# Value matmuls of 64-wide heads on four parts of the array, with an output projection split by sequence

## The reference

```python
q = (query @ Wq).reshape(Bq, Sq, 16, 64).transpose(0, 2, 1, 3)
k = (key @ Wk).reshape(Bq, Sq, 16, 64).transpose(0, 2, 1, 3)
v = (value @ Wv).reshape(Bq, Sq, 16, 64).transpose(0, 2, 1, 3)
scores = jnp.einsum('bhqd,bhkd->bhqk', q, k) / jnp.sqrt(64)
attn = jax.nn.softmax(scores, axis=-1)       # its window is wider than the 64 tokens
out = jnp.einsum('bhqk,bhkd->bhqd', attn, v)
return out.transpose(0, 2, 1, 3).reshape(Bq, Sq, 1024) @ Wo
...
x = x + jnp.tanh(g_xattn[3]) * _L3_xattn_ref(_layernorm(x), ctx_1024, ctx_1024, ...)
```

## Time and profile before

| what | value |
|---|---|
| median of 3 runs | 4556.94 us (4556.47 to 4561.93) |
| profiled execution | 4552.95 us, its span 4551.1 us |
| mean granted clock of TensorE | 0.866 |
| PE busy, matmuls | 3947.3 us (87%) |
| PE busy, weight loads | 3104.3 us (68%) |
| DVE busy | 3006.2 us (66%) |
| ACT busy | 1735.9 us (38%) |
| POOL busy | 764.9 us (17%) |

### The profile page before, as it was taken

One profiled execution on the slowest core, in us unless ns is written; L12 is line 12 of the kernel. 1 busy time (PEld: TensorE's weight loads), 2 busy tenths in 40 slices (PEclk: granted clock), 3 DMA queues, 4 the chain that ended last, 5 costly groups with the idle time before them and its releaser, 6 DMA issues.

```text
span 4551.1 us, 105680 instructions
## 1 busy us (share of the span) xinstructions
PE 3947.3 (87%) x36890; PEld 3104.3 (68%) x36890; DVE 3006.2 (66%) x9082; ACT 1735.9 (38%) x4156; POOL 764.9 (17%) x575
## 2 busy tenths in 40 slices
PE   6999978888886888889999999777737899999965
PEld 4888855555554555589999999655537777777754
DVE  4666657777775777766666666799861355555569
ACT  3555534444442344333333333222203344444421
POOL 1222221111110000011111111100171122222211
PEclk9999987777776677689999999888758999999975
DMA  3000010000001000000000000100015200000000
GB/s 124 8 7 8 7 23 6 6 6 6 6 7 65 16 16 15 15 6 0 0 0 0 0 0 3 44 12 12 6 39 191 98 12 12 9 12 12 10 13 26
DMA packets 102053, 97.04 MB, mean 21 GB/s; under 512 B 31664, under 2 KB 91056, under 8 KB 101296
## 3 DMA queue, kind: packets, MB, share of 16 engines
q1 hardware_dynamic: 97408, 76.94, 5.6%
q0 software_dynamic: 4096, 8.40, 0.6%
q10 hardware_dynamic: 432, 10.19, 0.6%
HBM read 46.97 MB, written 19.66 MB: 15 GB/s over the span
## 4 chain that ended last, share of the span: by engine, by line
PE 60%; DVE 18%; SPq 8%; issue 7%; POOL 2%; DMA 2%; ACT 1%; DVEq 1%; POOLq 0%; ACTq 0%
PE ps L768 54%; SPq L591 7%; PE ps L936 5%; DVE acc L1658 2%; DMA arena_a<-kT 1%; DVE o_sb L1637 1%; POOL scr L718 1%; PE ps L806 1%; DVE arena_b L1606 1%; POOL route L740 1%; DVE xn L1442 1%; DVE x_sb L1557 1%; DVE st L1401 1%; DVE mx L1527 1%; DVE vsmall L1614 1%
## 5 line engine op out<-in xcount | busy, mean ns | idle before, releaser
L768 PE MATMUL ps<-xcT,small 128*128 128x256 f32 x2176 | 610.1, 419 | 34.7 <-DMA xcT<-in_ctxT 25.4
L732 POOL TENSOR_TENSOR rstd<-veps,neghalf 128x2 f32<-128x2 f32 (+1 forms) x224 | 167.9, 749 | 2403.8 <-DVE veps L1434 2071.2
L768 PEld LDWEIGHTS ps<-xcT,small 128*128 128x128 f32 x2176 | 411.3, 204 | 233.3 <-issue 114.5
L768 PE MATMUL ps<-arena_b,qT 64*64 64x64 f32 (+3 forms) x11136 | 541.8, 242 | 21.6 <-DVE arena_b L1606 20.3
L1278 ACT ACTIVATE kT<-ps 128x256 f32<-128x256 f32 (+1 forms) x768 | 294.4, 383 | 623.6 <-PE ps L768 547.4
L768 PE MATMUL ps<-small,xcT 128*64 128x64 f32 (+5 forms) x3072 | 482.7, 384 | 51.4 <-DVE acc L1658 30.3
L768 PE MATMUL ps<-xhi,parts_a 128*128 128x256 f32 (+1 forms) x2112 | 500.4, 289 | 22.7 <-DVE qT L1687 22.7
L768 PEld LDWEIGHTS ps<-arena_b,qT 64*64 64x64 f32 (+3 forms) x11136 | 463.5, 149 | 58.4 <-issue 35.0
L1248 ACT ACTIVATE pT<-ps 128x512 f32<-128x512 f32 (+1 forms) x576 | 303.3, 571 | 467.0 <-PE ps L936 465.3
L1687 DVE TENSOR_TENSOR qT<-kT,ps 128x256 f32<-128x256 f32 (+1 forms) x768 | 316.8, 419 | 188.5 <-ACT kT L1278 181.0
L768 PE MATMUL ps<-xlo,parts_a 128*128 128x256 f32 (+1 forms) x1536 | 430.6, 280 | 0.0
(11 more groups left out here) (212 smaller groups left out, 6388.5 us busy)
## 6 DMA issues: line engine op xcount, KB each, us to landing
wbuf<-parts_b SPq DMA_DIRECT2D x39, 512.0 KB, 3.0
arena_a<-kT SPq DMA_DIRECT2D x1024, 8.0 KB
xcT<-in_ctxT SPq DMA_DIRECT2D x96, 128.0 KB, 2.1
xn<-scr SPq DMA_DIRECT2D x39, 128.0 KB, 2.2
scr_y<-acc SPq DMA_DIRECT2D x39, 128.0 KB, 2.9
scr<-vsmall SPq DMA_DIRECT2D x9, 512.0 KB, 13.3
ctx_sb<-in_ctx SPq DMA_DIRECT2D x32, 128.0 KB, 2.1
arena_a<-in_w ACTq DMA_DIRECT2D x1, 4096.0 KB, 12.4
```

The source lines that it names most:

```text
L732: pool.tensor_tensor(rstd[:, 0:n], veps[:, 0:n], neghalf[:, 0:n], ALU.pow).then_inc(s_rstd.sem, 1)
L768: return nc.tensor.matmul(o, lhsT, rhs, start=start, stop=stop, skip_group_check=True)
```

## The change

In both layers the value matmuls now run in one loop over heads, row half and sequence. The row half (which heads) decides the bank, and half and sequence together decide the output rows: for hb = 0 the rows are those of the half, for hb = 1 the other ones. So oT of the second sequence holds the even and odd heads with their row halves exchanged. ACT puts a bank into oT with two ACTIVATEs of 64x512 (one for each sequence) in place of one of 128x512. The output projection becomes two chains of 8 matmuls with 64 stationary columns each, one for each sequence; the second uses a copy of Wo with exchanged row halves, wo_swapped, which lies in arena_b. It is loaded by two DMAs ahead of most loads of the start, and for l3x by two DMAs in l2f ahead of the first tile's load; PE waits for it at the start of each of the two layers. The narrow layers, with the ones columns in their values, stay as they are.

```diff
+        wo_swapped = arena_b[:, 6144:7168]
...
+            def swap_wo(src, a, b):
+                for half in range(2):
+                    sp.dma_start(wo_swapped[half * S:(half + 1) * S, :],
+                                 src[(1 - half) * S:(2 - half) * S, a:b]).then_inc(s_swap, 16)
             n = TPG * 2
             sp.dma_start(x_sb[:, 0:n, :], x_v[:, 0:n, :]).then_inc(s_x0, 16)
             sp.dma_start(small[:, 0:FIRST_W], small_in[:, 0:FIRST_W]).then_inc(s_small, 16)
+            swap_wo(small_in, *SMALL_AT["l0x_wo"])
             sp.dma_start(x_sb[:, n:NT, :], x_v[:, n:NT, :]).then_inc(s_x, 16)
...
                 sp.wait_ge(s_lo, 16)
+                a = LATE.index("l3x_wo") * 1024
+                swap_wo(late_in, a, a + 1024)
                 load_tile(0)
...
                     pe.wait_ge(s_small, 16)
+                    pe.wait_ge(s_swap, 32)
...
                     pe.wait_ge(s_late, 16)
+                    pe.wait_ge(s_swap, 64)
...
                 pe.sem_inc(s_ready, 1)
-                blocks = [(0, hb) for hb in range(2)] if layer is L0X else [(i, hb) for i in range(4) for hb in range(2)]
-                for turn in ((0, 1), (1, 0)):
-                    halves = (0, 1) if turn == (0, 1) else (1, 0)
-                    for i, hb in blocks:
-                        for half in halves:
-                            j = turn[half]
-                            rows = slice(half * S, (half + 1) * S)
...
-                                last = mm(bank(banks[j])[rows, i * P + hb * S:i * P + (hb + 1) * S],
-                                          v_heads(layer, g.par)[rows, 2 * t + hb, 4 * j + i, :],
-                                          pT[rows, t, 4 * j + i, hb * S:(hb + 1) * S])
...
+                n = 2 if layer is L0X else 8
+                for c, half, hb in itertools.product(range(n), range(2), range(2)):
+                    rows = slice(half * S, (half + 1) * S)
+                    to = slice((half ^ hb) * S, ((half ^ hb) + 1) * S)
+                    w0, heads = 512 // n, 8 // n
+                    last = mm(bank(banks[half])[to, c * w0:(c + 1) * w0],
+                              v_heads(layer, g.par)[rows, 2 * t + hb, c, :],
+                              pT[rows, t, c * heads:(c + 1) * heads, hb * S:(hb + 1) * S])
+                    if (c, hb) == (n - 1, 1):
+                        last.then_inc(filled[banks[half]], 1)
...
                     b = take(ring, g, u)
+                    if chunks == 8:
+                        for c in range(8):
+                            for hb in range(2):
+                                toks = slice(hb * S, (hb + 1) * S)
+                                wo = w(layer.name + "_wo") if hb == 0 else wo_swapped
+                                last = mm(bank(b)[toks, 0:D], oT[:, t, c, toks], wo[:, c * D:(c + 1) * D],
+                                          start=c == 0, stop=c == 7)
+                        last.then_inc(filled[b], 1)
+                        return
...
                         b = wait_filled(ring, g, u + j)
-                        if layer is L0X:
-                            o = oT[:, t, 4 * j:4 * j + 4, :].rearrange("p i (b q) -> p b i q", b=2)
-                            i = bank(b).rearrange("p (b i q) -> p b i q", b=2, i=4)
-                        else:
-                            o = oT[:, t, 4 * j:4 * j + 4, :].rearrange("p c t -> p (c t)")
-                            i = bank(b)
-                        nc.scalar.activation(o, i, ACT.Copy).then_inc(drained[b], 1)
+                        for hb in range(2):
+                            rows = slice((j ^ hb) * S, ((j ^ hb) + 1) * S)
+                            last = nc.scalar.activation(oT[rows, t, :, hb * S:(hb + 1) * S],
+                                                        bank(b)[rows, :].rearrange("p (c q) -> p c q", q=S), ACT.Copy)
+                        last.then_inc(drained[b], 1)
```

More of the change, by code:

```diff
@@ L12 @@
+import itertools
 from contextlib import ExitStack
@@ L384, in build @@
         s_ones = ctx.enter_context(nc.semaphore("s_ones"))
+        s_swap = ctx.enter_context(nc.semaphore("s_swap"))
         s_rest = ctx.enter_context(nc.semaphore("s_rest"))
@@ L860, in heads_times_values @@
                 pe.sem_inc(s_ready, 1)
-                blocks = [(0, hb) for hb in range(2)] if layer is L0X else [(i, hb) for i in range(4) for hb in range(2)]
-                for turn in ((0, 1), (1, 0)):
-                    halves = (0, 1) if turn == (0, 1) else (1, 0)
-                    for i, hb in blocks:
-                        for half in halves:
-                            j = turn[half]
-                            rows = slice(half * S, (half + 1) * S)
-                            if layer is L0X:
-                                last = mm(bank(banks[j])[rows, hb * 256:(hb + 1) * 256],
-                                          v_heads(layer, g.par)[rows, 2 * t + hb, j, :],
-                                          pT[rows, t, 4 * j:4 * j + 4, hb * S:(hb + 1) * S])
-                            else:
-                                last = mm(bank(banks[j])[rows, i * P + hb * S:i * P + (hb + 1) * S],
-                                          v_heads(layer, g.par)[rows, 2 * t + hb, 4 * j + i, :],
-                                          pT[rows, t, 4 * j + i, hb * S:(hb + 1) * S])
-                            if turn == (1, 0) and (i, hb) == blocks[-1]:
-                                last.then_inc(filled[banks[j]], 1)
+                n = 2 if layer is L0X else 8
[8 more added lines that the diff above has]
+                        last.then_inc(filled[banks[half]], 1)
             def do(layer, item, g):
```

## The result

The changed kernel takes 4518.84 us (median of 4 runs, 4517.9 to 4519.67) against 4559.17 us for the kernel before beside it: ratio 0.9911, 95% interval 0.9894 to 0.9929. It is faster, by about 40 us where 76 were forecast, and 4519 lies above the stated range (4440 to 4515). The profiled executions took 4519.67 and 4552.95 us; their spans fell from 4551.1 to 4516.8, by 34.3.

What follows compares the result with a forecast made beforehand. TensorE's order of work was taken to bound l0x and l3x. Savings of 29 us in l0x and 51 in l3x, less 4 for loads, gave -76 us: median 4481 us, range 4440 to 4515.

Steps and rivals of the forecast that it cites:

- The value matmuls: In l0x and l3x: four array parts at once instead of two save 0.82 and 0.91 us a tile.
- The xcT wait in l0x: In l0x, ACT's xcT copy holds Q0 until +1.71 us from A0's start, leaving 0.16 of A0's 0.82 saving there.
- the duration of four copies: ACT's four 64x512 oT copies a tile last 2.06 us, +0.98 a tile, delaying A1 in both layers.
- The projection: Output projection as 16 matmuls of 64 stationary columns: taken as 0 change, between -0.1 and +0.16 us a tile.
- the cheap end: Output projection's lower bound: -0.1 us a tile, as shape-change costs fall away beside value projections of the same shape.
- dear end: Output projection's upper bound: 2.11 us a tile, +0.16 a tile and +20 us over 128 tiles.
- The loads: Two DMAs at the start and two in l2f delay waited-for loads 1.9 us each time: +4, bounds 0 and +8.
- the clock did not fall in the loops: Rival denied here: PE's granted clock falls in l0x, to 4699 us at clock 0.70; chance 0.04.
- the projections run one by one: Rival: output projection matmuls do not overlap because of weight loads, +250 us, 4731; chance 0.02.
- Rival 2: Value matmuls' four parts overlap less than in the scores, or projections cost +20 us: 4500 to 4520; chance 0.10.

Runs made afterwards that it cites:

- values alone: Kernel before with only the value matmuls on four parts, copies, projection and loads as before, un-mixing left out: 4474.95 us, ratio 0.9813.
- projection alone: Kernel before with only the output projection as 16 matmuls of 64 stationary columns: 4565.85 us, ratio 1.0008.
- split copies: Kernel before with each oT copy made as two of 64x512, upper and lower rows, all else as before: 4617.13 us, ratio 1.0122.
- orders alone: Kernel before with only two new orders of items, for l0x and l3x: 4560.85 us, ratio 1.0007.
- fence: Changed kernel, extra DMAs moved, with the earlier two turns and single copies, PE waiting on its own semaphore between turns: 4513.74 us, ratio 0.9899.
- order of the copies: Changed kernel with the four copies ordered bank 0 upper, bank 1 upper, bank 1 lower, bank 0 lower rows: 4546.38 us in a single run.
- adjacent output: Changed kernel with each 64x512 copy writing 512 adjacent elements instead of 8 runs of 64: 4522.06 us, ratio 0.9916.
- moved loads: Changed kernel with its four extra DMAs issued later, behind context columns and behind the last tile of l2f: 4516.27 us, ratio 0.9905.
- new order: Changed kernel with its four extra DMAs moved and another order of items in l0x and l3x: 4476.21 us, ratio 0.9817.

## Why the prediction missed its size

- **The value matmuls** were right: 1.02 to 1.09 us a tile (1.05 and 1.10 taken), and the order of parts that no row had shown does no harm. Alone they give 87 us.
- **The xcT wait in l0x** was right to 0.01 us (+1.71). ACT holds PE up there by the place of that copy in its order, not by its load (32.77 of 50 us): with F ahead of S1 and Q0 ahead of A0 the wait is gone.
- **The step that failed first is the duration of four copies**, "3 x 0.49 + 0.59 = 2.06". The spacing was read from copies of 128 partitions. Copies of 64 keep it only while the row half stays (0.48 to 0.50 us); each change of the half makes it 0.59 to 0.62, so four take 2.15, 2.27 and 2.42 us with one, two and three changes. In l0x A1 starts 0.22 us later than forecast. In l3x it is 0.32, of which the copies' later start and the hand-over make 0.05 each. That is 7 and 10 us over the 30 periods.
- **The projection** was taken as 0 and is +0.27 a period in l0x, or 8 us, from changes of shape around Q3; in l3x it is -0.09, so the cheap end was right there. The forecast had kept +20 us as its dear end.
- **The loads** were taken as +4, half of it at the start. The start alone is 4.3 us in this pair of traces, where 0.52 MB at 269 GB/s gave 1.9: the average over all queues did not give the delay of the context columns. Yet moving the loads gains at most 2.6 us in all, since an earlier start is partly handed back, and the half in l2f is not shown at all.
- **The ends of the layers** were left out. The forecast multiplied a period by 32, but A0 starts a period apart only 30 times. In the last two groups no projections stand between the value matmuls, so nothing covers the longer copies. From A0 of the last group but one to the opening of l0f it is 618.6 - 595.02 = 23.6 us in the kernel before and 614.4 - 585.39 = 29.0 in the changed one, 5.4 lost. There PE waits for the oT copies ahead of A1, first in the changed kernel, then in the kernel before:

```profile
585.39 1.09 PE L781 MATMUL ps<-pT,arena_a 64*64 64x256 f32 x16
589.43 1.98 PE L781 MATMUL ps<-pT,arena_a 64*64 64x256 f32 x16 [2.94 <-ACT oT L1273]
```

```profile
598.33 1.94 PE L768 MATMUL ps<-pT,arena_a 64*64 64x256 f32 x16 [1.37 <-ACT oT L1260]
```

  After the wait of 2.94 us the granted clock is 0.50 from 589.2 to 595.8, and A1 runs at half the speed of A0; in the kernel before it stays at 1.00 from 588 to 618. The last two A0s of l3x lie 4325.46 - 4309.58 = 15.88 us apart, where they were 13.45 apart: 2.4 of the 3.8 us that the end of the kernel lost. And l0f, which the change doesn't touch, is 4.0 us longer.

Summed against the forecast of -76: l0x without its last two groups +15, those two +5, l0f +4, l3x +11 (7 in its periods, most of the rest from the two groups that have none), loads and what lies around them +3, the end +4, which makes -34. Of the rivals, the clock did not fall in the loops (1.00), nor did the projections run one by one. Rival 2 has the measured time inside its 4500 to 4520, but by chance: the four parts overlap in full, and the projections alone cost about 6 us in all, not 20.

What stays open is l0f. It lasted 757.9 to 759.2 us in seven kernels (before, values alone, projection alone, split copies, orders alone, fence, order of the copies) and 763.1 to 763.6 in four (changed, adjacent output, moved loads, new order). All of the second four have the split copies with the gapped or adjacent exchange and no fence, but so has the order of the copies, which is in the first group. The clock goes with it: in the 60 us from l0f's opening the granted clock is 0.63 in each of the four and 0.69 or 0.72 in each of the seven. The kernel before and the changed one:

```profile
618.60:678.60 60.00, 42.12 (x174) 22.44 (x174) 39.53 (x139) 18.88 (x77) 14.93 (x8) 0.69 0.24 41
```

```profile
614.40:674.40 60.00, 42.43 (x158) 21.54 (x159) 38.04 (x133) 17.26 (x68) 14.94 (x8) 0.63 0.24 41
```

So l0f is longer where the clock is lower at the handover, but no run isolated what lowers it there, or that it accounts for the whole 4 us.

## What to carry to other kernels

When matmuls on the path get shorter, the wait moves to the copies that free their banks: lay out one period from the profile and check, item by item, which copy each new start waits for. Then change the order of items; the same two lists were worth 0 us before the change and 40 after it. Count the last groups by themselves, since nothing covers a copy there, and price an instruction on half the partitions in the order in which the halves will alternate.

## What the runs showed of the hardware

- ACT copies of 64x512 fp32 from a bank follow each other 0.48 to 0.50 us apart while the row half stays, and 0.59 to 0.62 where it changes, whether or not the bank changes too; the duration of one, 0.58 to 0.59 us in all three kernels, doesn't show it. Whether the output is adjacent or in runs of 64 elements makes no difference (2.27 us for four either way).
- Matmuls with 64 stationary columns on alternate column halves overlap: the output projection done as twice as many half-wide matmuls left the time nearly where it was (ratio 1.0008, 0.9999 to 1.0018). Going between them and full-array items costs about 0.1 us each way (+0.27 us a period where two such changes were added, -0.09 where as many were added as taken away).
- Waiting between the two turns of value matmuls on a semaphore of PE's own costs 0.41 us a tile (1.43 us against 1.02).
- A start of l0x 4.45 us earlier was worth 2.1 us at its end: the first 16 records ran 6.20 us instead of 5.18, and the granted clock was 0.50 from 54.5 to 57.8 us instead of 1.00.
